# Layer 2 of a graph network: residual and bias added into the accumulators early, layer norm in place, last source block over 20 quads instead of 24

## The reference

```python
src, dst, norm = _gcn_norm(edge_index, n)          # norm = dinv[src] * dinv[dst]
h = _gcn_conv(x, W1, b1, src, dst, norm, n)        # segment_sum((x @ W)[src] * norm, dst) + b
h = _gcn_conv(h, W2, b2, src, dst, norm, n)
h = _gcn_conv(h, W3, b3, src, dst, norm, n)
out = layernorm(x + h)                             # (r - mean) / sqrt(var + 1e-5), per row
```

## Time and profile before

| | |
|---|---|
| median of 3 runs | 2347.21 us (2343.35 to 2349.53) |
| profiled execution, its own time | 2344.56 us |
| span of its profile | 2342.7 us |
| layer 1: first gather to last gather | 1018.0 to 1637.0 us |
| layer 2: first gather to last gather | 1654.5 to 2298.6 us |
| mean granted TensorE clock | 0.933 of full |

### The profile page before, as it was taken

How to read it: one execution, slowest core, us unless ns; L and a number is a source line. 1 busy time by engine, 2 the same in 40 slices (tenths; PEclk the granted TensorE clock), 3 DMA queues, 4 the chain that set the end, 5 groups by cost and what they waited for, 6 DMA issues and landing times.

```text
span 2342.7 us, 32832 instructions
## 1 busy us (share of the span) xinstructions
PE 2024.8 (86%) x10242; PEld 1157.4 (49%) x10242; DVE 1490.5 (64%) x3665; ACT 803.4 (34%) x1521; POOL 1611.0 (69%) x1698
## 2 busy tenths in 40 slices
PE   6655777899989988779999999998899999999764
PEld 6321223454445433246666566664466666666431
DVE  8435776777767764355555555556656666666787
ACT  0602553444434433233333333334333333323110
POOL 0257777777777777647777777777577777777760
PEclk7766899999999998999999999999899999999876
DMA  8556888888888888758888888889688888898883
GB/s 281 211 167 181 277 271 249 249 251 248 245 254 286 277 253 249 232 159 243 249 248 250 258 269 269 266 264 320 200 242 262 262 260 280 273 287 285 282 279 113
DMA packets 288153, 585.68 MB, mean 250 GB/s; under 512 B 73204, under 2 KB 132529, under 8 KB 287985
## 3 DMA queue, kind: packets, MB, share of 16 engines
q0 software_dynamic: 132784, 434.04, 60.9%
q1 hardware_dynamic: 155200, 149.59, 19.3%
HBM read 516.40 MB, written 67.06 MB: 249 GB/s over the span
## 4 chain that ended last, share of the span: by engine, by line
PE 34%; POOL 12%; issue 6%; DVE 2%; DMA 2%; ACT 0%; DVEq 0%; ACTq 0%
PE ps L1299 25%; POOL ring L972 12%; PE ps L1186 7%; PE ps L1197 1%; DMA ring<-y_dram,kept 1%; PE ps L1198 1%; DVE acc L2115 0%; PE ps L1354 0%; DVE ln L1973 0%; DMA out_dram<-row_sb 0%; DVE acc L1918 0%; DMA onehot<-a_dram 0%; DVEq L1914 0%; DVE y_words L1964 0%; DVE y_words L1971 0%
## 5 line engine op out<-in xcount | busy, mean ns | idle before, releaser
L972 POOL DMA_INDIRECT ring<-y_dram,kept x1650 | 1582.4, 959 | 588.0 <-issue 492.3
L1186 PE MATMUL ps<-ring,onehot 128*32 128x512 f32 x3300 | 467.7, 634 | 80.0 <-DMA ring<-y_dram,kept 78.7
L2115 DVE SCALAR_TENSOR_TENSOR acc<-ps,acc 128x512 f32<-128x512 f32 x494 | 341.1, 690 | 277.7 <-PE ps L1299 261.6
L1299 PE MATMUL ps<-dense_first,wide_a 128*128 128x512 f32 x1144 | 321.3, 402 | 14.0 <-DVE dense_first L2086 6.4
L1299 PEld LDWEIGHTS ps<-dense_first,wide_a 128*128 128x128 f32 x1144 | 213.8, 191 | 103.7 <-issue 26.7
L1299 PE MATMUL ps<-dense_next,wide_a 128*128 128x512 f32 x820 | 238.6, 399 | 8.0 <-ACT wide_a L1542 6.7
L1542 ACT CAST wide_a<-onehot 128x512 fp32r<-128x512 uint8 (+1 forms) x297 | 171.3, 593 | 202.4 <-PE ps L1299 124.2
L1918 DVE SCALAR_TENSOR_TENSOR acc<-ps,mask,acc 128x512 f32 x280 | 197.2, 746 | 67.9 <-issue 65.7
L1299 PE MATMUL ps<-dense_first,y_rows 128*128 128x512 f32 x756 | 211.7, 401 | 2.5 <-DVE dense_next L2086 1.7
L1885 DVE TENSOR_TENSOR onehot<-ps,kept 128x128 f32<-128x128 f32 x417 | 119.4, 287 | 145.6 <-PE ps L1186 143.2
L1503 ACT CAST ring<-ps 128x490 uint8<-128x490 f32 x228 | 154.2, 692 | 138.9 <-PE ps L1256 137.4
(11 more groups left out here) (289 smaller groups left out, 2302.7 us busy)
## 6 DMA issues: line engine op xcount, KB each, us to landing
onehot<-a_dram SPq DMA_DIRECT2D x456, 64.0 KB
ring<-y_dram,kept POOLq DMA_INDIRECT x1650, 4.1
y_dram<-acc SPq DMA_DIRECT2D x99, 256.0 KB, 10.1
a_dram<-ring SPq DMA_DIRECT2D x19, 784.0 KB, 6.0
acc<-in_x_dram SPq DMA_DIRECT2D x1, 12288.0 KB
y_dram<-acc SPq DMA_DIRECT2D x12, 1024.0 KB, 11.0
out_dram<-row_sb SPq DMA_DIRECT2D x48, 256.0 KB
w_sb<-in_x_dram SPq DMA_DIRECT2D x24, 256.0 KB, 4.0
```

The source lines that it names most:

```text
L972: pool.indirect_dma_start(ring[:, s, :], None, y_dram[layer], bass.IndirectOffsetOnAxis(ap=rows, axis=0)).then_inc(done, 16)
L1186: mm = pe.matmul(ps[k * WIDE:(k + 1) * WIDE, g % BANKS, :], wide_hot[:, r, k, :], ring[:, r * CPQ + k, :], start=opens, stop=closes, tile_ ...
L1299: mm = pe.matmul(ps[:, bank, :], wide_slots[n % WIDE_SLOTS][:, P * k:P * (k + 1)], y_parts[(TILES * (layer - 1) + tile) % YSLOTS][:, part, :],
L2115: dve.scalar_tensor_tensor(out=rows, in0=ps[:, UNIT_BANKS[n % len(UNIT_BANKS)], :], scalar=0.5, in1=rows, op0=ALU.mult, op1=ALU.add).then_ ...
```

## The change

In layer 2 every tile's x and bias go into its accumulator early. Since h = dinv_sum * acc + b, the new `add_residual` adds (x + b) / dinv_sum to acc, and the norm then runs on acc itself: a row scaled by s has its mean and its deviation scaled by s, so eps is scaled to EPS / dinv_sum^2 (`eps_sum`, per row and tile). The 49 residuals are spread over quads 2 to 102, one every second quad, those of tiles that serve as a resident source only after that source's split (`residual_quads`). x comes through the same two buffers, loaded two residuals ahead. `begin_norm` loses its first two instructions, `finish_norm` writes in place and its wait for `o_stored` goes; the stores read acc. The last block's units stand in quads 105 to 121 instead of 101 to 120, and the inner 209 in quads 2 to 104. On ScalarE `root_turn` moves behind `high_part` and `widen_a` within a quad.

```diff
-    NORM_STEPS = 5
+    NORM_STEPS = 3
+    LAST_WINDOW = 20
+    RES_FROM = 2
-    UNITS_TO = [0, DENSE_QUADS - 6, DENSE_QUADS - 24]
+    UNITS_TO = [0, DENSE_QUADS - 6, DENSE_QUADS - LAST_WINDOW]
+    def residual_quads():
+        due = {t: at for at, late, t in FINISH[LAYERS - 1]}
+        left, found = set(range(TILES)), []
+        for j in range(TILES):
+            q = RES_FROM + j * (UNITS_TO[LAYERS - 1] - RES_FROM) // TILES
+            t = min((t for t in left if residual_split(t) < q), key=lambda t: (t == TILES - 1, due.get(t, DENSE_QUADS), t))
+            left.remove(t)
+            found.append((q, t))
+        return found
...
+            def load_x(j):
+                t = RESIDUAL[j][1]
+                if j > 1:
+                    sp.wait_ge(x_added, j - 1)
+                if t < TILES - 1:
+                    sp.dma_start(x_bufs[j % 2], node_rows(x, t, 0, P)).then_inc(x_turn_loaded[j % 2], 16)
...
-                    load_x(k + 2)
                     sp.wait_ge(o_ready, k + 1)
-                    sp.dma_start(node_rows(out, t, 0, P), row_sb[:, :]).then_inc(o_stored, 16)
+                    sp.dma_start(node_rows(out, t, 0, P), tile_of(t)).then_inc(o_stored, 16)
...
-                    if layer == LAYERS - 1:
-                        for t in finished_at(layer, q - 1)[-1:]:
-                            root_turn(TURN_OF[layer][t])
                     for tile in splits_at(layer, q):
                         high_part(layer, tile)
                     for u in units_at(layer, q + 1):
                         widen_a(layer, u)
+                    if layer == LAYERS - 1:
+                        for t in finished_at(layer, q - 1)[-1:]:
+                            root_turn(TURN_OF[layer][t])
...
+            def scale_sums():
+                mark(dve.reciprocal(inv_sum, dinv_sum[:, :]))
+                caught_up()
+                link(dve.scalar_tensor_tensor(out=eps_sum, in0=inv_sum, scalar=EPS, in1=inv_sum, op0=ALU.mult, op1=ALU.mult))
+
+            def add_residual(j, groups, units):
+                t = RESIDUAL[j][1]
+                buf = x_bufs[j % 2]
+                if j == 0:
+                    dve.wait_ge(y_stored, 16 * TILES * (LAYERS - 1))
+                dve.wait_ge(x_turn_loaded[j % 2], 16 * (j // 2) + 16 * (len(LAST_PARTS) if t == TILES - 1 else 1))
+                dve.tensor_tensor(buf, buf, ps[:, BIAS_BANK, :], ALU.add).then_inc(x_biased, 1)
+                dve.wait_ge(added, 2 * groups)
+                dve.wait_ge(dense_added, units)
+                dve.wait_ge(split_ready, TILES * (LAYERS - 2) + residual_splits(j))
+                dve.wait_ge(x_biased, j + 1)
+                dve.scalar_tensor_tensor(out=tile_of(t), in0=buf, scalar=inv_sum[:, t:t + 1], in1=tile_of(t),
+                                         op0=ALU.mult, op1=ALU.add).then_inc(x_added, 1)
...
-                dve.scalar_tensor_tensor(out=h, in0=tile_of(t), scalar=dinv_sum[:, t:t + 1], in1=ps[:, BIAS_BANK, :],
-                                         op0=ALU.mult, op1=ALU.add).then_inc(norm_step, 1)
...
-                dve.tensor_tensor(h, h, x_bufs[k % 2] if last is None else last_x[last], ALU.add).then_inc(norm_step, 1)
...
-                if last != 1 and k > 0:
-                    dve.wait_ge(o_stored, 16 * k)
-                dve.tensor_scalar(row_sb[:, :] if last is None else last_row[last][:, :], h, ln[:, at + 6:at + 7], ln[:, at + 10:at + 11],
+                dve.tensor_scalar(tile_of(t), tile_of(t), ln[:, at + 6:at + 7], ln[:, at + 10:at + 11],
                                   ALU.subtract, ALU.mult).then_inc(o_ready, 1)
...
+                    if layer == LAYERS - 1:
+                        for j in residuals_at(q):
+                            add_residual(j, max(GROUP_AT[layer], g), units_before(layer, 0) + units)
```

More of the change, by code:

```diff
@@ L234, in resident0, with residual_split, residuals_at, residuals_by @@
         return source0(k) >= EARLY_DENSE and SPLIT0_QUAD[k // PAIR] < touch_quad(0, source0(k))
+    def residual_split(t):
+        k = (t - FIRST_SOURCE) % TILES
+        return SPLIT_QUAD[LAYERS - 1][k] if resident(LAYERS - 1, k) else -2
+    def residual_quads():
[7 more added lines that the diff above has]
+        return found
+    RESIDUAL = residual_quads()
+    assert RESIDUAL[-1][1] == TILES - 1 and all(q < at for q, t in RESIDUAL for at, late, u in FINISH[LAYERS - 1] if u == t)
+    def residuals_at(q):
+        return [j for j, (at, t) in enumerate(RESIDUAL) if at == q]
+    def residuals_by(q):
+        return sum(at < q for at, t in RESIDUAL)
     LOADED = [[k for k in range(TILES) if layer == 0 or not resident(layer, k)] for layer in range(LAYERS)]
@@ L828, in load_y @@
                 sp.dma_start(y_rows[n % YSLOTS][:, 1, :], node_rows(y_dram[layer], source(tile), 0, P)).then_inc(y_loaded[n % YSLOTS], 16)
[L830 to L834, removed]
-                    for a, rows in parts_of(t):
[L836 to L842, removed]
+            def load_x(j):
[4 more added lines that the diff above has]
+                    sp.dma_start(x_bufs[j % 2], node_rows(x, t, 0, P)).then_inc(x_turn_loaded[j % 2], 16)
+                else:
+                    for a, rows in parts_of(t):
+                        sp.dma_start(x_bufs[j % 2][a:a + rows, :], node_rows(x, t, a, rows)).then_inc(x_turn_loaded[j % 2], 16)
             def store_rows(layer, t):
@@ L886, in dense_layer @@
                             load_a(layer, u)
-                    if layer == LAYERS - 1 and UNIT_QUAD[layer][UNITS - DENSE] + 1 == q:
-                        load_last_x()
+                    if layer == LAYERS - 1:
+                        for j in residuals_at(q - 1):
+                            if j + 2 < TILES:
+                                load_x(j + 2)
                     for t in finished_at(layer, q - (1 if layer == LAYERS - 1 else 0)):
@@ L902, in last_tiles @@
                         for a, rows in parts_of(t):
-                            sp.dma_start(node_rows(out, t, a, rows), last_row[k][a:a + rows, :]).then_inc(o_stored, 16)
+                            sp.dma_start(node_rows(out, t, a, rows), tile_of(t)[a:a + rows, :]).then_inc(o_stored, 16)
             with order_holds(sp):
@@ L1903, in split_slots, with add_group @@
                                   ALU.subtract).then_inc(slots_split, 1)
-            def add_group(g, units=0):
+            def add_group(g, units=0, residuals=0):
                 dve.wait_ge(placed, g + 1)
@@ L1912, in add_group @@
                     dve.wait_ge(dense_added, units)
+                if residuals > 0:
+                    dve.wait_ge(x_added, residuals)
                 own = own_of(g)
@@ L1972, in begin_norm @@
                 dve.wait_ge(norm_step, done + 2)
[L1973 to L1981 removed]
+                dve.tensor_scalar(ln[:, at + 8:at + 9], ln[:, at + 7:at + 8], eps_sum[:, t:t + 1], None, ALU.add).then_inc(norm_step, 1)
@@ L2105, in add0_unit, with add_unit @@
                                          op0=ALU.mult, op1=ALU.add).then_inc(dense0_added, 1)
-            def add_unit(layer, u, groups):
+            def add_unit(layer, u, groups, residuals=0):
                 n = units_before(layer, 0) + u
@@ L2119, in dense_layer @@
                 units = 0
+                if layer == LAYERS - 1:
+                    scale_sums()
                 low_part(layer, 0)
@@ L2126, in dense_layer @@
                     g, a = QUAD[n]
+                    residuals = residuals_by(q) if layer == LAYERS - 1 else 0
                     if q > 0:
                         for u in units_at(layer, q - 1):
-                            add_unit(layer, u, max(GROUP_AT[layer], g - (1 if a == 0 else 0)))
+                            add_unit(layer, u, max(GROUP_AT[layer], g - (1 if a == 0 else 0)), residuals)
                             units += 1
@@ L2132, in dense_layer @@
                     if a == 0 and q > 0:
-                        add_group(g - 1, units_before(layer, 0) + units)
+                        add_group(g - 1, units_before(layer, 0) + units, residuals)
                     if layer == LAYERS - 1:
                         for t in finished_at(layer, q - 1)[-1:]:
-                            finish_norm(TURN_OF[layer][t])
+                            finish_norm(TURN_OF[layer][t], t)
                     done = finished_at(layer, q)
```

39 lines of the change are left out of this document (17 added, 22 removed).

## The result

The changed kernel takes 2314.20 us, the median of 4 runs (2310.48 to 2317.75), against 2346.32 us (4 runs, 2343.35 to 2349.53) for the kernel before on the same chip: a ratio of 0.9857, 95% interval 0.9837 to 0.9877. It is 32.1 us faster, where the prediction had 36.5 us and a time of 2310. The profiled execution took 2315.01 us, with a span of 2313.1.

A forecast was written before the change was run, and what follows sets the result against it. VectorE was taken to bound layer 2's end; afterwards gathers would. Last gather at 2282.0, 8.4 us to the last split, 15.8 to the end: 2306.2, 36.5 us less; 2347.2 - 36.5, rounded to 2310 us, range 2296 to 2325.

The forecast's parts named there:

- The bound moves from VectorE to the gathers: Layer 2's end: VectorE would need 4.4 us a quad against 5.07 for the gathers, which then set the pace.
- The inner window: Inner units over four more quads: TensorE brings quad 105 at 2193.5 us, the gathers at 2195.0, the later limit.
- rival 1: Layer 2's end keeps 6.4 us a quad, set by TensorE's half clock and the chain; 14 us won, 2333; chance 0.10.
- VectorE's work in the end: Quads 106 to 122: norms at about 1.75 us, adds, one-hot steps and splits sum to 75 us on VectorE.
- Contention: Layer 2's gathers slowed by 27 residuals and 27 scalings at 0.22 us each, 5.9 us in all; upper bound 15.7.
- Rival 2: Each of 27 residuals and 27 scalings blocks a gather for its whole length: 33.5 us instead of 5.9, 2338; chance 0.06.
- Behind the last gather: Quad 122's last gather to last full split: 8.4 us; from that split to the span's end: 15.8, before 18.6.
- Costed at nothing: Small setup instructions, 49 residuals taking VectorE to about 75% in the steady stretch, x loads and SyncE's queue: no time.
- the third: Steady stretch: late residuals on VectorE make TensorE wait for banks, 74 us if wholly exposed, giving 2384; chance 0.07.
- The fourth: Layer 2's gathers at layer 1's pace without contention: 5.3 + 5.9 us less, 2299; counted within the forecast's 0.77.

The follow-up runs named there:

- residual_psum_in: The changed kernel with each residual's second instruction taking the bias from PSUM instead of x from SBUF, leaving x out of the result; 2303.51 us, ratio 0.9822.
- halves_psum: The changed kernel with each residual in two half tiles, x + bias written to a free PSUM half bank and added from there; 2301.70 us, ratio 0.9817.
- extra_one_sbuf: The changed kernel with an unused VectorE addition behind each residual, one operand in SBUF and one in PSUM; 2310.80 us, ratio 0.9849.
- window16: The changed kernel with the last block over 16 quads instead of 20; 2317.51 us, ratio 0.9866.
- early_only: The changed kernel with the last block still over 24 quads; 2313.45 us, ratio 0.9855.
- window_only: The kernel before with only the last block changed, to 20 quads from 24; 2346.97 us, ratio 0.9992.
- in_place_late: The kernel before with the norm written back into the accumulator and no out-store wait, x and bias still added in the norm; 2337.39 us, ratio 0.995.
- after_again: The changed kernel without an edit, run again on the second chip; 2689.03 us, ratio 0.994 to the kernel before there.

## Why the prediction was right

**The bound moves from VectorE to the gathers: right.** GpSimd's waits for the ring fell from 21.9 to 3.0 us in layer 2, TensorE's waits for gathered rows in the end rose to 18.3 us, and the kernels that quicken the gathers (residual_psum_in, halves_psum) are shorter by 8.6 us of gathers, while one that loads VectorE further (extra_one_sbuf) is not longer. Between the forecast and its rivals this is what the runs on the first chip decide; on the second they leave it open.

**The inner window: nearly right.** I put quad 105 at 2195 us. It came at 2207.86: 5.9 us are the later start of layer 2, and (2202.20 - 1660.33) / 423 = 1.281 us a gather, not the 1.266 that I kept up to there, makes another 423 x 0.015 = 6.3; I had charged contention only to the layer's total. The longer window, to which rival 1 gave 11.4 us, is worth 0.8 us alone and nothing beside the rest.

**VectorE's work in the end: right.** I summed 75 us for quads 106 to 122; between 2208 and 2298 us VectorE is busy for 70.2 of 90 us. The price of a norm, 1.75 us, is measured at 1.77 (1.12 and 0.65 above). From 2288.6 us to the last full split's end at 2297.9 VectorE has one gap, of 0.27 us, so it is by little that it no longer sets the pace, as said; window16 shows it take over again.

**Contention: the size right by luck, the mechanism wrong.** I added 5.9 us for 27 residuals and 27 scalings at 0.22 us. The busy time of all gathers rose from 475.7 to 481.0 us, by 5.3. First to last they take 630.3 us, where the prediction's rule gives 493 x 1.266 + 5.9 = 630.0. But the 0.22 us came from a wrong reading: I put all of layer 2's 4.8 us over layer 1 down to 22 norms. In the trace of before the gathers up to the first stall lose 5.2 us under dense splits (L2086), 2.5 us in layer 1, and only 1.8 us under L1971. After, 13.5 us are lost where 8.6 were, 6.0 of them under residuals, which replace L1971's 2.6; that the difference comes to what I had is chance. Nor is it a small price on each: a gather that starts under a VectorE instruction with two operands in SBUF loses up to 0.5 us, and most gathers meet none. Rival 2's full lock is thus real for each gather it meets and wrong as a sum, since it let every residual and scaling meet one. The Trainium skill, "SBUF — State Buffer", section "Who interferes with whom", says that a `tensor_scalar` may take the shared port pair for its whole length, and with L2023 and the gather at 2245.07 (1.19 us) the trace agrees. The page also infers that an addition with two operands in SBUF leaves the making of a gather's descriptors alone; the gathers of 1.40 and 1.46 us above, and 6.0 us less under the residuals in residual_psum_in, say otherwise here.

**Behind the last gather: right, with two small errors that nearly cancel.** From the 492nd gather to the last full split I had 8.4 us, measured 2297.21 - 2288.13 = 9.1. The rows landed for the sum at 2292.33, 4.2 us after the gather began instead of 5.0, but then VectorE's line of norms stood before the split, 4.9 us instead of 3.4. From the split to the end I had 15.8, measured 15.9.

**The start of layer 2: the term that I didn't have.** The 492nd gather was predicted for 2282.0 and started at 2288.13, but layer 2's first gather started at 1660.33 instead of 1654.46: measured from there it is 627.8 us against 627.5. I took the start from one execution of before. Layers 0 and 1 are the same code in most kernels here, and their profiles give 1655.5 (early_only), 1657.4 (window16), 1657.7 (window_only) and 1659.1 us (in_place_late), so it scatters by about 6 us. From first gather to end of span the kernel lost 688.2 - 652.8 = 35.4 us, by 1.1 less than the 36.5 predicted; the profiled execution of after began its layer 2 late, that of before early. early_only has the change's code and starts early, in_place_late has not and starts late, so nothing speaks for the change moving the start; so few profiles don't rule it out.

**Costed at nothing: right.** Neither x loads nor SyncE's queue show: the DMA rate in the inner stretch rose from 266 to 275 GB/s, VectorE has no wait for a DMA among its waits of the inner stretch, and ScalarE's waits for the loads of counts, which share SyncE's queue with x, are 55.4 us in layer 2 where they were 58.8. VectorE went to 73% there, 75 predicted; 79% in extra_one_sbuf cost nothing either, which says how much room there was.

**The rivals.** The first fell with window_only (2346.97 us for an expected gain of 11 to 14), the second with the mean gather of 0.974 us, the third with early_only and extra_one_sbuf, neither of which is slower than the kernel after. The fourth, gathers without contention, 2299 us, is nearly reached by halves_psum with 2301.7, by an edit which the change doesn't make.

## What to carry to other kernels

When the end of a layer is bound by an engine that is otherwise idle a third of the time, move its work to where it is idle, and read from the trace which engine will set the pace then; here that was a DMA-issuing GpSimd at 76% busy which is never free, since 0.3 us of issue follow each gather. Once gathers from GpSimd's queue set the pace, look at the operands of VectorE's instructions beside them: with one operand of the 49 residual additions in PSUM instead of SBUF, no gather was slowed under them any more (6.0 us less), and in halves_psum that was worth its extra work on VectorE. On the second chip no such gain was seen. A stretch that was shortened alone (the window) won nothing, since the engine that bounds it had the same work to do. And the shares of the chain that ended last are no proof of a bound: kernels of equal time had 31% and 17% of it in gathers.

## What the runs showed of the hardware

An indirect gather issued by GpSimd that starts within a 128x512 VectorE instruction with two operands in SBUF, or within a 128x512 `tensor_scalar` from SBUF to SBUF, ends 0.82 us after that instruction, up to 1.46 us instead of 0.946; in the kernel after this holds for 52 of the 56 that start more than 0.18 us before its end, and the other 4 start within 0.07 us of its beginning. Beside an instruction with one operand in PSUM gathers keep their 0.95 us, but for three of up to 1.05. I had not expected that so few collide, 55 gathers of 494, with 13.5 us lost between them. And the same kernel takes 2346 us on one chip and 2707 on another, where GpSimd, mostly together with VectorE, stops 48 times in layer 2 of after_again, for 1.9 us in the median; the change is worth 1.4% on the first and 0.6% on the second.
